# A one-core decoder layer: matmuls without a reader in TensorE's pauses behind the last head

## The reference

```python
# 1: self-attention, 16 heads of 128
q, k, v = x @ Wq, x @ Wk, x @ Wv ; q, k = rmsnorm(q, wq), rmsnorm(k, wk)
scores = q @ k.T / sqrt(128) - dist * slope[h]      # causal
y = rmsnorm(softmax(scores) @ v, subln_w)
x = layernorm(x + concat(y) @ Wproj)
# 2: mixing by a cross-attention map of 256 x 256 that comes from the context alone
attention = softmax((ctx @ xWq.T + bq) @ (ctx @ xWk.T + bk).T)
x = layernorm(x + x @ attention.T)
# 3: feed-forward with activations in 8 bits and weights in 3 values
def bitlinear(x, w): return quant_act(x) @ quant_weight(w).T   # quant_act: per token, max|x| / 127
h = sigmoid(bitlinear(x, w_gate)) * bitlinear(x, w_up)         # 1024 wide
x = layernorm(x + bitlinear(h, w_down))
```

## Time and profile before

| what | value |
|---|---|
| runs, us | 437.57, 438.52, 438.9 |
| profiled execution, us | 438.66 |
| its span, us | 436.9 |
| mean granted TensorE clock, whole span | 0.962 |
| TensorE matmul busy | 402.6 us (92%) |
| DVE, ACT, POOL busy | 296.4, 282.1, 181.2 us |
| from TensorE's last instruction of the main loop (L541, ends 400.07 us) to the end of the span | 36.8 us |

### The profile page before, as it was taken

The page is one execution under the profiler, slowest core; times in us unless marked ns, Lnnn a source line. Parts: engine busy times, 40 slices in busy tenths (PEclk is TensorE's granted clock), DMA queues, the critical chain, the costliest instruction groups (busy, mean ns, idle before and its releaser), DMA issues.

```text
span 436.9 us, 8760 instructions
## 1 busy us (share of the span) xinstructions
PE 402.6 (92%) x2610; PEld 369.3 (85%) x2620; DVE 296.4 (68%) x920; ACT 282.1 (65%) x797; POOL 181.2 (41%) x283
## 2 busy tenths in 40 slices
PE   4699999999999999999999999999999999985644
PEld 3599998999999998999999999999999999974312
DVE  4678778876677676667485676667584776666563
ACT  2287866777777676777666677677665777762132
POOL 3666766544344333335353433335263433332101
PEclk9699999999999999999999999999999999999585
DMA  7999100000000000000010000000000000000000
GB/s 193 278 331 294 50 1 2 2 1 14 2 24 2 2 2 2 1 2 0 2 41 22 2 0 3 2 1 2 0 26 2 1 2 1 2 2 0 25 0 24
DMA packets 21663, 14.84 MB, mean 34 GB/s; under 512 B 1649, under 2 KB 21361, under 8 KB 21617
## 3 DMA queue, kind: packets, MB, share of 16 engines
q1 hardware_dynamic: 20800, 13.90, 11.0%
q10 hardware_dynamic: 816, 0.39, 0.3%
HBM read 13.24 MB, written 1.05 MB: 33 GB/s over the span
## 4 chain that ended last, share of the span: by engine, by line
PE 89%; DVE 5%; issue 2%; POOL 1%; ACT 1%; DMA 1%; POOLq 0%; DVEq 0%; ACTq 0%
PE ps L499 31%; PE ps L541 12%; PE ps L509 7%; PE ps L522 6%; PE ps L516 5%; PE ps L521 3%; PE ps L528 3%; PE ps L530 3%; PE ps L529 3%; PE ps L549 3%; PE ps L462 2%; PE ps L472 1%; PE ps L450 1%; PE ps L617 1%; PE ps L595 1%
## 5 line engine op out<-in xcount | busy, mean ns | idle before, releaser
L372 POOL TENSOR_TENSOR qk_rstd<-qk_sum,minus_half 128x2 f32<-128x2 f32 x128 | 93.0, 726 | 114.6 <-DVE qk_sum L793 114.1
L499 PE MATMUL ps<-w_hi,xT_hi 128*128 128x384 f32 x256 | 101.6, 399 | 3.9 <-DVE qk_n L787 2.0
L793 DVE TENSOR_REDUCE qk_sum<-sq 128x2 f32<-128x258 f32 x128 | 53.9, 421 | 73.7 <-ACT sq L688 70.0
L688 ACT ACTIVATE sq<-ps 128x256 f32<-128x256 f32 x128 | 49.5, 386 | 73.5 <-PE ps L499 73.4
L499 PE MATMUL ps<-w_hi,xT_lo 128*128 128x384 f32 x256 | 87.2, 342 | 0.0
L367 POOL TENSOR_TENSOR y_rstd<-y_sum,minus_half 128x2 f32<-128x2 f32 x64 | 47.4, 741 | 95.9 <-DVE y_sum L990 93.5
L499 PE MATMUL ps<-w_lo,xT_hi 128*128 128x384 f32 x256 | 87.0, 341 | 0.0
L787 DVE TENSOR_TENSOR qk_n<-ps,qk_rstd 128x256 f32<-128x256 f32 x128 | 53.9, 421 | 33.4 <-POOL qk_rstd L372 33.1
L541 PE MATMUL ps<-wp,yT 128*128 128x256 f32 x256 | 65.9, 380 | 0.1
L499 PEld LDWEIGHTS ps<-w_hi,xT_hi 128*128 128x128 f32 x256 | 49.3, 193 | 7.8 <-DVE w_hi L957 2.3
L499 PEld LDWEIGHTS ps<-w_lo,xT_hi 128*128 128x128 f32 x256 | 49.4, 193 | 1.3 <-POOL w_lo L327 0.3
(11 more groups left out here) (163 smaller groups left out, 778.1 us busy)
## 6 DMA issues: line engine op xcount, KB each, us to landing
wp<-in_L_attn_Wproj SPq DMA_DIRECT2D x4, 512.0 KB, 5.8
x_sb<-in_x SPq DMA_DIRECT2D x4, 256.0 KB, 3.1
ff_raw<-in_L_ffn_w_gate SPq DMA_DIRECT2D x1, 1024.0 KB, 7.1
ff_raw<-in_L_ffn_w_up SPq DMA_DIRECT2D x1, 1024.0 KB, 9.7
w_raw<-in_L_attn_Wq SPq DMA_DIRECT2D x4, 256.0 KB, 7.1
w_raw<-in_L_attn_Wk SPq DMA_DIRECT2D x4, 256.0 KB, 6.5
w_raw<-in_L_attn_Wv SPq DMA_DIRECT2D x4, 256.0 KB, 6.0
ff_raw<-in_L_ffn_w_down SPq DMA_DIRECT2D x1, 1024.0 KB, 8.7
```

What stands on the lines that cost most here:

```text
L372: pool.tensor_tensor(qk_rstd[:, t, :], qk_sum[:, t, :], minus_half[:], ALU.pow).then_inc(s_rs[t], 1)
L499: last = pe.matmul(ps[:, t, 0:W3], xa[:, b % 2, k, tok], wa[:, h, k * W3:(k + 1) * W3], start=(i == 0), stop=(i == len(parts) - 1))
L688: act.activation(sq[:, t, :, 0:D], ps[:, t, 0:2 * D].rearrange("p (a d) -> p a d", a=2), ACT.Square).then_inc(s_sq[t], 1)
L793: dve.tensor_reduce(qk_sum[:, t, :], sq[:, t], AX.X, ALU.add).then_inc(s_ss[t], 1)
```

## The change

In the tail a function `keep_busy(bank, count)` is added and called four times. Each of its matmuls takes the bf16 identity as the stationary operand and 512 columns of the gate weights as the moving one, and writes a whole PSUM bank. Nothing reads that bank before it is written anew. There are 18 + 16 + 20 + 4 = 58 of them. Two waits on `s_sig` are added, since banks 0 and 1 are read by ACT's tanh before.

```diff
+            def keep_busy(bank, count):
+                for _ in range(count):
+                    pe.matmul(ps[:, bank, :], ident16[:], wgT[:, 0, 0:BANK], start=True, stop=True)
+
             pe.wait_ge(s_side_out, len(JOB))
+            keep_busy(3, 18)
             for t in range(TT):
                 pe.wait_ge(s_x1, tiles_done(LAST, t))
...
                 last.then_inc(s_xm, 1)
+            keep_busy(3, 16)
             for t in range(TT):
                 pe.wait_ge(s_xq, tiles_done(LAST, t))
...
                         last.then_inc(done, 1)
+            pe.wait_ge(s_sig, 1)
+            keep_busy(0, 20)
             for t in range(TT):
                 pe.wait_ge(s_hq, 2 * LAST + t + 1)
                 for f in range(FC):
                     last = pe.transpose(bank16(4 * t)[:, f * P:(f + 1) * P], hq[:, t, f * P:(f + 1) * P], ident16[:])
                 last.then_inc(s_th, 1)
+                if t == 0:
+                    pe.wait_ge(s_sig, 2)
+                    keep_busy(1, 4)
                 pe.wait_ge(s_hT, t + 1)
```

## The result

The changed kernel took 433.57, 434.14, 433.98 and 433.82 us, median 433.9; the kernel before had 438.31 as the median of four runs by then. The ratio is 0.990, with a 95% interval of 0.9883 to 0.9917: one per cent faster. The forecast was 433.5, the range 432.6 to 436.0. The profiled execution took 433.57 us, with a span of 431.8.

What follows compares the result with a forecast made beforehand. It took TensorE's clock, falling to half after two pauses in the last 33 us, as the loss. Gains of 1.92 + 1.57 + 1.72 - 0.05 = 5.16 us off 438.66 gave 433.5 us, range 432.6 to 436.0.

Steps and rivals of the forecast that it cites:

- First stage: Behind the main loop: 18 matmuls keep the clock full, eight mixing rows take 1.9 instead of 3.7 us; gain 1.92 us.
- Second stage: Behind the mixing: 16 matmuls keep tile 0's feed-forward at full clock, DVE's search starts at 414.00; adds 1.57 us.
- Third stage: Last stage: 20 and 4 matmuls speed both tiles' transposes (0.43 each) and tile 1's down projection (0.86); gain 1.72 us.
- The sum: Whole tail: 1.92 + 1.57 + 1.72 - 0.05 = 5.16 us off 438.66 gives 433.5.
- The rival by which the clock falls in the last stage: Last stage: the clock falls anyway, 1.72 lost and up to 0.6 us paid, 435.2 to 435.9 us; chance 0.15.
- The slower rival: Pauses of the tail: added matmuls run late, at half clock 0.427 us each, giving 441 to 447 us; chance 0.04.

Runs made afterwards that it cites:

- the new order alone: The kernel before with the last stage reordered (ACT rounds tile 1 before copying tile 0; TensorE turns tile 1 before tile 0's down projection): 436.3 us.

## Why the prediction was right, and where it was not

- **First stage, 1.92 us.** The transposes of xq start at 410.45 instead of 412.28: 1.83 us. Neither call costs anything here, where I had taken off 0.05: the transposes of x1 start at 404.24, before at 404.33, and those of tile 1 wait for DVE's L839 at 404.38; the 16 of the second end as xq comes. The 0.09 us that are missing are DVE's: it takes up tile 1 at 407.40 and not 407.35, and needs 0.04 us more from there to xq (407.40 to 410.10, before 409.27 to 411.93).
- **Second stage, 1.57 us.** DVE's search starts at 414.02 instead of 417.49, 3.47 us in all and 1.64 in this stage. That DVE hides tile 1's faster matmuls held: 6.6 us from there to the transposes of hq in both kernels.
- **Third stage, 1.72 us.** The last addition starts at 427.08 instead of 432.16: 5.08 us in all, 1.61 here. Most of the missing 0.1 is the last down projection, 1.12 us instead of 1.04: the clock fell in it. That tile 1's transposes would be released by DVE is in the chain.
- **The sum.** 5.16 us forecast, 5.09 between the two profiled executions (438.66 to 433.57). The medians differ by 4.4 only. The profiled execution of before lies 0.35 us above its median and that of after 0.33 below. The sum was worked out for the one profiled execution, and I took it that the clock fell in much the same way in the others. Their clocks say no: of the 31 runs of the kernel before that were made beside the experiments, 16 have a mean granted clock of 0.962 to 0.966 and took 438.41 to 438.89 us, and 15 have 0.972 to 0.977 and took 437.55 to 438.39. The profiled execution is of the first kind (0.962). So about half of the runs had 0.5 us less to win, and the forecast fits the medians less well than the rows. Where in the kernel the second kind has its clock, no rows of it show. The mean over a run holds its first 40 us too, where the profiled executions have 0.91 to 1.00 with no clear effect on when the tail begins. The kernels with the third and fourth calls alone and with the new order alone show one way to gain, the clock coming back for a while behind the mixing, but only 0.1 to 0.2 us of it.
- **The rival by which the clock falls in the last stage** got 0.15 and did not come about in the profiled execution but for the last 0.2 us of the work, though its mechanism is real: without the fourth call it did. Its price, 1.72 us and up to 0.6 more, is above what the rows show: the tails are 1.0, 1.2 and 0.8 us longer without the third call, the fourth, and both. In the first and the last, the clock was back before the last down projection.
- **The slower rival** never applied: the added matmuls ran at full clock, 0.216 us each, and ended in time. That late ones delay the work behind them is real: ten too many made it 1.27 us late, and the four at half clock without the third call took 1.71 us on the path.
- **What the calls are worth.** The first and second carry most of the change: 2.0 and 1.5 us are lost without them by the medians, 2.4 and 1.6 by the tails. The prediction had the third stage worth 1.72 us, and as a difference to the kernel before it is (1.61 in the rows; by the third and fourth calls alone 1.3 in the medians and 1.7 in the tail). As the value of these two calls in the changed kernel it is too much: 0.15 in the medians, 0.8 in one execution's tail.

## What to carry to other kernels

Read the granted clock by stage: where a stage behind a pause runs at half and lies on the path, work without a reader in the pause can pay for itself, and its price is zero only up to the due time of the work behind it. Count it from the spacing of like matmuls in the trace and stop short. Then look for what the faster stage waits for now: here another order of ACT's and TensorE's last work gave 2.6 us more, beside 4.4 from the clock. And read the granted clock of every run, not only of the profiled one: half of the runs of the kernel before were of another kind than the one whose rows the sum came from.

## What the runs showed of the hardware that I had not expected

- Bf16 transposes keep TensorE's clock at 2.4 GHz as matmuls of 512 columns do (72 in 4.19 us, clock 1.00).
- Pauses shorter than the 4.3 and 4.7 us of before go with a fall: 3.3 us (fall 2.3 us in), 1.9 us (fall 1.5 us after work had begun again), and pauses of 0.7 and 1.1 us around 0.62 us of transposes (fall 0.2 us after work had begun again). The same kernel escapes it in some executions (433.61 beside 435.28 to 435.58, clock 0.993 beside 0.981 to 0.988).
- The clock also comes back in a stage with pauses of about 1.1 us: at half from 418.6, back at 425.4, with TensorE busy for 3.94 of the 5.10 us from 420.3 on. It does not always: without the fourth call it stayed at half from 422.5 to the end of the last down projection, with TensorE busy for 4.62 of the 6.00 us from 422.2 on. What decides is not shown.
